# The expert part of an audio block as a pipeline over experts: 24 row gathers first, then one behind each store or add

## The reference

```python
    def _L0_ffn_ref(x, Wr, W1, b1, W2, b2):
        E, F, CAP = (8, 512, 1024)
        ...
        logits = x_flat @ Wr
        probs = jax.nn.softmax(logits, axis=0)
        vals, idx = jax.lax.top_k(probs.T, C)
        selected = x_flat[idx]
        h = jax.nn.gelu(jnp.einsum('ecd,edf->ecf', selected, W1) + b1[:, None, :], approximate=False)
        out_e = jnp.einsum('ecf,efd->ecd', h, W2) + b2[:, None, :]
        weighted = vals[..., None] * out_e
        output = jnp.zeros_like(x_flat).at[idx.reshape(-1)].add(weighted.reshape(-1, Dd))
    h = _L0_tok_ref(x)
    h = h + _L0_attn_ref(_layernorm(h, axis=-1), ...)
    h = h + _L0_ffn_ref(_layernorm(h, axis=-1), ...)
```

## Time and profile before

| | us |
|---|---|
| three runs | 594.83, 597.33, 600.74 (median 597.33) |
| profiled execution, time | 593.88 |
| its span | 592.0 |
| busy in the span: PE, DVE, POOL, ACT | 416.8, 406.5, 300.3, 292.0 |

### The profile page before, as it was taken

One profiled execution on the slowest core, in us unless ns is written; L12 is line 12 of the kernel. 1 busy time (PEld: TensorE's weight loads), 2 busy tenths in 40 slices (PEclk: granted clock), 3 DMA queues, 4 the chain that ended last, 5 costly groups with the idle time before them and its releaser, 6 DMA issues.

```text
span 592.0 us, 12234 instructions
## 1 busy us (share of the span) xinstructions
PE 416.8 (70%) x4045; PEld 333.7 (56%) x4045; DVE 406.5 (69%) x1614; ACT 292.0 (49%) x560; POOL 300.3 (51%) x213
## 2 busy tenths in 40 slices
PE   6897889999888888999323333300399989996900
PEld 6787778966877788965212222200276657775700
DVE  4876978799488978799666588813876858846100
ACT  3786940067688950067655500210278657685400
POOL 0466840038488840048000017774436687788774
PEclk9998999999899999999655555555599989998965
DMA  7689606599868506599999901111112354443332
GB/s 167 135 193 276 150 13 148 138 252 243 195 151 154 96 12 154 148 289 267 286 325 322 320 16 45 47 53 35 27 28 76 64 76 70 74 68 41 29 30 22
DMA packets 86117, 77.45 MB, mean 131 GB/s; under 512 B 15022, under 2 KB 82930, under 8 KB 85810
## 3 DMA queue, kind: packets, MB, share of 16 engines
q1 hardware_dynamic: 68674, 64.52, 42.1%
q0 software_dynamic: 10368, 8.40, 9.9%
q10 hardware_dynamic: 7024, 3.89, 2.8%
HBM read 52.27 MB, written 39.39 MB: 155 GB/s over the span
## 4 chain that ended last, share of the span: by engine, by line
PE 37%; DVE 19%; issue 12%; POOL 9%; DMA 8%; ACT 7%; another core or an unknown queue 4%; SPq 1%; ACTq 1%; DVEq 0%; POOLq 0%
PE banks L1008 8%; POOL out L1858 7%; PE banks L1035 5%; PE banks L934 5%; DMA xin<-in_x 4%; PE banks L1152 4%; PE banks L1165 4%; PE banks L1045 3%; ACT xn L685 3%; PE banks L1078 3%; PE banks L920 2%; DVE xn L1532 2%; DVE place L1635 1%; ACT hid L676 1%
## 5 line engine op out<-in xcount | busy, mean ns | idle before, releaser
L1233 DVE BATCH_NORM_STATS2 stats<-hid 120x6 f32<-120x128 f32 (+1 forms) x512 | 104.9, 278 | 19.9 <-ACT hid L676 19.4
L1844 POOL DMA_INDIRECT hid<-kept,index x64 | 66.4, 1038 | 100.1 <-DVE index L1639 81.5
L1858 POOL DMA_INDIRECT out<-hid,index x56 | 88.8, 1587 | 26.7 <-issue 16.9
L934 PE MATMUL banks<-const,xt 128*120 128x128 f32 x512 | 75.1, 293 | 11.1 <-ACT xt L671 10.6
L780 ACT ACTIVATE xt<-banks 128x480 f32<-128x480 f32 x64 | 36.3, 571 | 84.7 <-PE banks L1035 83.5
L934 PEld LDWEIGHTS banks<-const,xt 128*120 128x120 f32 x512 | 64.9, 194 | 19.7 <-ACT xt L671 13.5
L1766 POOL TENSOR_TENSOR small<-small,powers 120x16 f32<-120x16 f32 (+2 forms) x18 | 47.9, 2663 | 46.6 <-DVE small L1251 46.6
L1165 PEld LDWEIGHTS banks<-w_ring,xn 128*128 128x128 f32 x512 | 61.9, 199 | 4.4 <-issue 4.1
L1834 POOL TENSOR_TENSOR small<-small,powers 120x16 f32<-120x16 f32 x15 | 43.2, 2902 | 41.4 <-DVE small L1251 36.1
L1165 PE MATMUL banks<-w_ring,xn 128*128 128x128 f32 x512 | 62.4, 282 | 1.0 <-issue 1.0
L1008 PE MATMUL banks<-xn,ring 122*120 122x128 f32 x512 | 58.6, 276 | 6.3 <-DMA xn<-s 3.1
(11 more groups left out here) (222 smaller groups left out, 694.2 us busy)
## 6 DMA issues: line engine op xcount, KB each, us to landing
kept<-out SPq DMA_DIRECT2D x1, 15008.0 KB, 51.5
xin<-in_x SPq DMA_DIRECT2D x28, 480.0 KB, 6.7
out<-hid SPq DMA_DIRECT2D x14, 960.0 KB, 11.1
w_ring<-in_L_ffn_W SPq DMA_DIRECT2D x16, 256.0 KB
ring<-toeplitz SPq DMA_DIRECT2D x32, 112.5 KB
toeplitz<-ring SPq DMA_DIRECT2D x6, 545.0 KB, 11.4
out<-hid SPq DMA_DIRECT2D x2, 784.0 KB
xin<-in_x SPq DMA_DIRECT2D x4, 384.0 KB
```

Of the source, the lines that this page charges most:

```text
L934: mm = pe.matmul(banks[0:L, 2 + n % 4, i * D:(i + 1) * D], xt[:, n % 2, i, :], cut["basis_t"], start=True, stop=True)
L1233: ins = dve.bn_stats(stats[:, slot, b, :], hid[:, bass.ds(c * HB + b, 1), :].rearrange("p a k -> p (a k)"))
L1844: pool.indirect_dma_start(found[:, n, :], None, kept, bass.IndirectOffsetOnAxis(ap=index[:, n:n + 1], axis=0)).then_inc(found_in[e], 16)
L1858: pool.indirect_dma_start(rows, at_rows, adds[:, n, :], None, compute_op=ALU.add, oob_is_err=True, bounds_check=ROWS * FRAMES - 1).then_in ...
```

## The change

The expert part is put into another order on all engines. DVE's `extract` is split into `number` and `rank_rows`, and the blocks of the eight experts are written one behind another, so that the first moments come behind pair 1, and pairs 2 and 3 stand between the answers of experts 0 to 2. PE and ACT follow it. The ranks of experts 4 to 7, with the tables of pairs 2 and 3, all use PSUM bank 7, so each of them waits until DVE has read the one before (`row_used`). The reduction of `far` is cut into 8 pieces, one in each of the last 8 counting rounds. `weights_of` runs once for each expert. POOL issues 24 gathers (three experts) first, and each expert's `add` carries the gathers of the expert three further on: one behind each of the first six stores or adds, two behind the last. The stores and adds lose `bounds_check` and `oob_is_err`; the gathers had none before.

```diff
-FOUND_FIRST = 54
-WEIGHED_AFTER = {3: (3, 5), 5: (5, 7), 6: (7, 8)}
-FOUND_BETWEEN = 2
+FOUND_FIRST = 24
+NEAR_PIECES = 8
+NEAR = SEG // NEAR_PIECES
+RANK_COLS = 4 * (L + 2)
...
-        def offsets_bank(pair):
-
-            return 0 if pair < PAIRS - 1 else 5
+        def offsets_of(pair):
+
+            if pair < 2:
+                return banks[:, 0, 16 * pair:16 * pair + 10]
+            return banks[:, 7, RANK_COLS + 10 * (pair - 2):RANK_COLS + 10 * (pair - 1)]
+
+        def steps_bank(pair):
+
+            return 1 + pair if pair < 2 else 7
 
         def rank_bank(e, q):
 
-            return 6 if q and e < E - 1 else 7
+            return 6 if q and e < 4 else 7
...
-                               banks[:, 1 + pair, 0:4 * (L + 2)], ACT.Copy).then_inc(steps_ready, 1)
+                               banks[:, steps_bank(pair), 0:RANK_COLS], ACT.Copy).then_inc(steps_ready, 1)
...
-            for pair in range(PAIRS - 1):
-                own_steps(pair)
+            own_steps(0)
             act.wait_ge(far_out, 32)
             act.wait_ge(nearest_ready, 1)
             act.activation(far, far, ACT.Exp, scale=-1.0, bias=sc[:, 10:11], accum_out=sc[:, 4:5]
                            ).then_inc(sum_ready, 1)
             act.activation(sc[:, 7:8], sc[:, 7:8], ACT.Gelu)
+            own_steps(1)
             normalise_rows(0)
             turned(0)
-            own_steps(PAIRS - 1)
             for e in range(E):
                 gelus(2 * e)
-                if e == 1:
-                    weights_of(1, 2)
                 gelus(2 * e + 1)
-                if e == 2:
-                    weights_of(2, 3)
+                if e in (1, 2):
+                    own_steps(e + 1)
+                weights_of(e, e + 1)
                 if e < E - 1:
                     normalise_rows(e + 1)
-                if e == 0:
-                    weights_of(0, 1)
-                if e < E - 1:
                     turned(2 * e + 2)
-                if e in WEIGHED_AFTER:
-                    weights_of(*WEIGHED_AFTER[e])
...
+                if pair > 1:
+                    pe.wait_ge(row_used, 4 * pair)
                 ranked = rank[:, 4 * pair:4 * pair + 4, :]
-                into = banks[:, 1 + pair, 0:4 * (L + 2)]
+                into = banks[:, steps_bank(pair), 0:RANK_COLS]
...
-                if e:
-                    pe.wait_ge(row_used, 2 * e + q - (0 if q and e == E - 1 else 1))
+                if e or q:
+                    pe.wait_ge(row_used, 2 * e + q - (1 if e < 4 else 0))
...
+                    elif f == FC - 1:
+                        pe.wait_ge(spread_taken, 1)
...
                 if n == 1:
-                    pe.wait_ge(row_used, 2 * E - 2)
+                    pe.wait_ge(row_used, 8)
...
-            for pair in range(PAIRS):
-                if pair == 2:
-                    pe.wait_ge(peak_ready, 1)
...
-                    ffn_turn(0)
-                offsets(pair)
-                differences(pair)
-                for e in (2 * pair, 2 * pair + 1):
-                    if e < E - 1:
-                        for q in range(2):
-                            ranks(e, q)
-            for e in range(E):
...
+            offsets(0)
+            differences(0)
+            ranks(0, 0)
+            peaks_of_group()
+            ranks(0, 1)
+            ranks(1, 0)
+            ranks(1, 1)
+            offsets(1)
+            sum_of_group()
+            differences(1)
+            ranks(2, 0)
+            scales_of_experts()
+            ranks(2, 1)
+            ffn_turn(0)
+            ranks(3, 0)
+            up(0)
+            ranks(3, 1)
+            up(1)
+            down(0)
+            down(1)
+            ffn_turn(2)
+            up(2)
+            offsets(2)
+            up(3)
+            differences(2)
+            ranks(4, 0)
+            down(2)
+            ranks(4, 1)
+            down(3)
+            ranks(5, 0)
+            ranks(5, 1)
+            ffn_turn(4)
+            up(4)
+            offsets(3)
+            up(5)
+            differences(3)
+            ranks(6, 0)
+            down(4)
+            down(5)
+            ranks(6, 1)
+            ffn_turn(6)
+            up(6)
+            ranks(7, 0)
+            up(7)
+            ranks(7, 1)
+            down(6)
+            down(7)
+            for e in range(4, E):
+                ffn_turn(2 * e)
                 up(2 * e)
-                if e == 0:
-                    ranks(E - 1, 0)
                 up(2 * e + 1)
-                if e == 3:
-                    ranks(E - 1, 1)
                 down(2 * e)
-                if e < E - 1:
-                    ffn_turn(2 * e + 2)
                 down(2 * e + 1)
 
...
-                dve.tensor_reduce(sc[:, 0:1], far, AX.X, ALU.min).then_inc(dve_own, own.one())
+                dve.tensor_reduce(sc[:, 0:1], near[:, :], AX.X, ALU.min).then_inc(dve_own, own.one())
...
+                    if phase:
+                        dve.tensor_reduce(near[:, columns(i, 2, k, 1)], far[:, columns(i, 2 * NEAR, k * NEAR, NEAR)],
+                                          AX.X, ALU.min).then_inc(dve_own, own.one())
...
-            def extract(pair):
+            def number(pair):
...
-                cutoff = banks[:, 5, 2 * pair:2 * pair + 2].unsqueeze(2).broadcast_to([P, 2, 2 * L])
+                cutoff = cut_offs[:, 2 * pair:2 * pair + 2].unsqueeze(2).broadcast_to([P, 2, 2 * L])
...
+
+            def rank_rows(pair):
...
-                if pair == 3:
-                    dve.wait_ge(spread_done, 2)
-                    dve.tensor_copy(spread[:, :, :].rearrange("p a b -> p (a b)"),
-                                    banks[:, 4, 2 * P:2 * P + 2 * E]).then_inc(dve_own, own.one())
...
-            for pair in range(PAIRS - 1):
-                if pair == 2:
-                    nearest_of_partitions()
-                extract(pair)
-                if pair == 2:
-                    nearest_of_experts()
-                choose(2 * pair)
-                choose(2 * pair + 1)
+            def take_scales():
+
+                dve.wait_ge(spread_done, 2)
+                dve.tensor_copy(spread[:, :, :].rearrange("p a b -> p (a b)"),
+                                banks[:, 4, 2 * P:2 * P + 2 * E]).then_inc(spread_taken, 1)
+                dve.wait_ge(spread_taken, 1)
+
+            dve.tensor_copy(cut_offs[:, :], banks[:, 5, 0:E]).then_inc(dve_own, own.one())
+            dve.wait_ge(dve_own, own.all())
+            number(0)
+            rank_rows(0)
+            nearest_of_partitions()
+            choose(0)
+            nearest_of_experts()
+            choose(1)
+            number(1)
+            rank_rows(1)
             softmax_scales()
             moments_of_found(0)
-            extract(PAIRS - 1)
-            choose(E - 2)
+            choose(2)
+            take_scales()
+            choose(3)
+            score_of_found(0)
             moments_of_found(1)
-            score_of_found(0)
-            for e in range(E):
-                if e == 1:
-                    score_of_found(1)
-                    moments_of_found(2)
-                if e == 2:
-                    score_of_found(2)
-                    choose(E - 1, (0,))
-                    moments_of_found(3)
-                if e == 3:
-                    score_of_found(3)
-                    moments_of_found(4)
-                    score_of_found(4)
+            answer(0, 0)
+            number(2)
+            answer(0, 1)
+            rank_rows(2)
+            choose(4)
+            choose(5)
+            score_of_found(1)
+            answer(1, 0)
+            answer(1, 1)
+            moments_of_found(2)
+            score_of_found(2)
+            number(3)
+            rank_rows(3)
+            moments_of_found(3)
+            choose(6, (0,))
+            answer(2, 0)
+            choose(6, (1,))
+            answer(2, 1)
+            choose(7)
+            score_of_found(3)
+            moments_of_found(4)
+            for e in range(3, E):
                 answer(e, 0)
                 answer(e, 1)
-                if e == 3:
-                    choose(E - 1, (1,))
-                if e >= 3 and e + 2 < E:
+                if e + 1 < E:
+                    score_of_found(e + 1)
+                if e + 2 < E:
                     moments_of_found(e + 2)
-                    score_of_found(e + 2)
...
+                ahead = FOUND_FIRST + e * SLOT_TILES
+                more = range(ahead, min(ahead + SLOT_TILES, E * SLOT_TILES))
...
                     if e:
-                        pool.indirect_dma_start(rows, at_rows, adds[:, n, :], None, compute_op=ALU.add, oob_is_err=True,
-                                                bounds_check=ROWS * FRAMES - 1).then_inc(added, 16)
+                        pool.indirect_dma_start(rows, at_rows, adds[:, n, :], None, compute_op=ALU.add
+                                                ).then_inc(added, 16)
                     else:
```

(13 more changed lines are left out.)

35 lines of the change are left out of this document (20 added, 15 removed).

## The result

Nineteen runs of each kernel:

| | before | after |
|---|---|---|
| median of the timed runs, us | 595.54 (590.74 to 600.74) | 600.87 (598.00 to 604.21) |
| profiled execution, time / span | 593.88 / 592.0 | 602.18 / 600.4 |

The account below looks back on a forecast made before the run. POOL was taken as the bound from the second expert's adds on, DVE before the first store. Span 581.0, with 1.9 around it 582.9, 4 for clock restarts: 587; plus 3.4 for timed runs: 590 us, range 580 to 610.

Parts of the forecast that it names:

- The hold: DVE's 24 us wait for finished ranks of pair 2 (10.15 and 13.70), releaser unknown; forecast gone, its return given 0.25.
- my span of 581.0: Whole kernel: last add's issues end at 573.2, with POOL bound from expert 3 on, plus 7.8 us behind the last issue.
- The schedule without it: Expert part without the hold: first store at 394.6, first add at 423.6, second expert's adds at 450.6.
- the first rival: The hold returns; at the ranks of experts 4 and 5 it shifts add(1) by 24 us: 611; any return 0.25.
- The stages with gathers: POOL's adds with gathers between them: 8 x (1.82 + 1.25) = 24.6 us a stage, POOL the bound from there on.
- The bounds checks: Checks dropped from stores and adds: 0.04 us for each of 64, 2.2 us, already in the add's 1.82.
- The clock: PE restarts at 1.2 GHz, three before 450: 4 us; rival that the clock returns late, 594 to 606, chance 0.17.
- The tail: Landing and closing behind POOL's last issue: 7.8 us, taken from the profile before.
- The 3.4 us between profile and timed runs: Three timed runs' median of 597.33 against the profiled 593.88, added to 587 to give 590.
- The gain itself: Stores start 50 us earlier; 24 + 10 of it go into POOL's waits and gathers no longer in front.
- The rival with the hold at experts 2 and 3: The hold strikes these experts' ranks, DVE's other waits cover some 7 us: about 603; any return 0.25.

Follow-up runs that it names:

- the paced kernel: The changed kernel with a 400-column POOL memset behind gathers n = 8 to 31 and each store of expert 0: 589.71 us, 0.9943.
- the run beside POOL: Separate kernel computing nothing of the reference: PE's product groups in nine sections beside different POOL work; 24 gathers in a row cost 23.4 us, 24 adds 0.0.
- the two paced ones in the old order: The kernel before with a POOL memset behind gathers n = 8 to 53, of 400 columns: 587.46 us, 0.9864; of 128 columns: 583.35 us, 0.9842.
- the held sections: Parts of the kernels computing nothing of the reference in which engines were slowed beside POOL's transfers, such as 24 gathers at 1.25 us: 23.4 us lost.
- second kernel: Separate kernel, products beside 24 transfers in each of seven sections, with memsets, bursts or 512-column products: 0.0 us lost at 1.67, 10 in bursts of 12.

## Why the prediction was wrong, by its steps

- **The hold.** This is the step that failed. I gave 0.48 to a kernel without it and 0.25 to its return, for want of a cause: "POOL gathers without a pause and PE does ranks" stood in the text as a coincidence, and it was half of the mechanism. Both of my grounds against were wrong. That the ranks of pair 0 were not held fits the need for several us of gathers in quick succession first. Those of pair 1 ran 11.5 to 16 us after the first gather and were not held either; the first gap also came later where an engine issued fewer instructions (18.3 us beside 256-column products, 11.2 beside 128-column ones), but that this is the reason here was not shown. And "the flood is now 24 long" overlooked that 24 are enough and that stores with gathers between them are a second flood, 16 long at 1.28 us. It came back in both, at the ranks of experts 3 and 4: DVE waited 10.3 us at each instead of 24 in one place, of which 6.3 and 8.0 lie behind the end of the ranks. In the terms of my sum: DVE reached the second expert's adds at 465.30 instead of 450.6, 14.7 of the 19.4 us between my span of 581.0 and the measured 600.4.
- **The schedule without it** was right to a microsecond, as the paced kernel shows: first store 394.6 forecast, 394.04 there (399.87 with the hold); first add 423.6, 423.46 (436.58); second expert's adds 450.6, 451.26 (465.30). So the hold and its aftermath cost 13.0 us up to the first add, and 14.7 by the second; counted from the first gather of each profile (352.89 changed, 351.09 paced) the two kernels differ by 11.3 and 12.2. Small slips are in my sums: 415.8 + 8 is 423.8 and not 423.6, 423.6 + 26.2 + 1 is 450.8 and not 450.6, and in the first rival 582.9 + 24 + 3.4 is 610.3 and not 611.
- **The stages with gathers.** Forecast 3.07 us for an add with a gather and 24.6 for a stage; measured 3.19 (an add beside gathers takes 1.59 to 1.60, the gather 0.98) and 26.3, 25.9, 25.6 in the paced kernel. The plain add's 1.56 could not be carried over. +4.0 us to the last issue, less 1.0 of landing waits (2.02 and 1.98 for 2.5 each).
- **The bounds checks**: 2.2 us forecast, at the issue of each transfer, and 0 found there; the 1.0 us is in the two landings, where I had left 2.5 each.
- **The clock**: the 4 us for restarts, for which I had no row, are not to be seen; the marks above were met without them, with the clock at 0.95 between 380 and 413 in the paced kernel. It did fall in the changed kernel after the holds, 0.71 between 413 and 445 with PE busy for 12.64 of 32 us, and in the run beside POOL from 1.00 to 0.56. The page "TensorE: Matmul & The Clock Gate" of the Trainium skill, Part 1, says that the throttled state is the default and that activity releases it; both rows agree.
- **The tail**: 7.8 us forecast behind the last issue, 9.1 measured, and 9.0 in the paced kernel. The kernels in the new order have 9.0 to 9.5, the two paced ones in the old order 7.7 and 7.8. Its cause was not looked for. It is not the checks: with them the changed kernel has 9.0.
- **The 3.4 us between profile and timed runs**: they came from three runs. Over nineteen the kernel before is 1.7 above its profile, and the changed one 1.3 below its own (600.87 against 602.18).
- **The gain itself.** "Its gain is that stores start 50 us earlier, and 24 + 10 of it go into POOL's waits and into the 30 gathers": I made POOL's sum for the new kernel and never for the old one. With the same durations it gives for the kernel before 351.7 + 64 x 1.25 + 8 x 1.26 + 56 x 1.82 + 32.6 + 7.8 = 584.1, and its span was 592.0. So 7.9 of the 11 us between 592.0 and my 581.0 were durations taken too short (the mean gather there is 1038 ns and the mean add 1587, with 0.3 of gap each, where I had 1.25 and 1.82), and the change without any hold was worth 3.3 us of waits, 32.6 against 24.3 + 5. The 24 us of hold before lay for the most part under gathers that POOL had to issue anyway: freed of it at the price of 46 memsets (21.0 us of POOL's time), that kernel gains 8 us (0.9864), and 9 (0.9842) with 10.5 us of memsets, not 24.

The rival with the hold at experts 2 and 3 gave 603, and 600.9 came: the mechanism was in the text and its chance was too low. That the number fits so well is partly luck. The rival had 17 us for the hold where about 13.5 were lost by the second expert's adds (14.7, less the 1.2 of a later first gather), nothing for what came behind (4.7 us: longer stages and tail, less the shorter landings), and 3.4 for the timed runs, which came out 1.3 below the profile.

## What to carry to other kernels

Indirect transfers from POOL in a quick row (more than 6; held at a pitch of 1.44 us, not at 1.67) hold up PE, DVE and ACT at each of their instructions; put them between work of POOL that is due anyway, or spread them with a short memset, before reordering anything around them. When one engine issues a fixed list of transfers to the end, compare its waits in both versions: a start that is 45 us earlier is worth only what its waits shrink. A wait whose releaser the profile can't name, on an instruction that is long in the trace, is a cause to be found before a change is costed.

## What had not been expected of the hardware

The recorded issue of an instruction and its completion can lie far apart: eight rank products recorded as over at 381.4 released DVE at 387.7. POOL is late now and then as well: a gather came 3.42, 3.69 and 3.54 us late in three of the held sections. That this is the hold is not shown, since one came 3.54 us late also while PE ran without a gap (second kernel, at 284.54). What it is that each instruction pays was not shown. The steps of 0.7 us are alike on PE, DVE and ACT, and long instructions are spared. The page "NOTIFIC — the notification-queue block" of the Trainium skill, section 7.1, says, in part as an inference, that the block which takes the engines' records holds its producers up rather than lose a record inside. If the transfers slowed its writes, these two facts would follow, and a kernel whose instructions are not recorded would not be held. No run here shows it: every one has its granted clock and span on record. So what the hold costs an execution that is not recorded is open too.
